# Edge attention of a graph network: scores spread as rows of 512 edges, maxima of two heads at once

## The chip, the cores and the metric

One Trainium2 chip, one of its cores. The metric is the device time of one execution, in microseconds (us).

## The reference, cut to what matters

The program is four stacked graph networks over 3,125 nodes of 128 features (a GAT of three layers, an edge MLP, a GATv2 of two layers, a GCN of two layers). The change lies in the GATv2 alone, whose layer is:

```
xl = (h @ Wl + bl).reshape(N, H, HD); xr = (h @ Wr + br).reshape(N, H, HD)
e = leaky_relu(xl[src] + xr[dst], 0.2)
score = einsum('ehd,hd->eh', e, att)
m = segment_max(score, dst, num_segments=N)
ex = exp(score - m[dst])
den = segment_sum(ex, dst, num_segments=N)
out = segment_sum(ex / (den[dst] + 1e-16) * xl[src], dst, num_segments=N)
```

The reference is given 100,000 edges, sorted by their target `dst`; H is 4 heads, HD 32 features of each.

## The kernel before, in words

Edges are sorted once into NG = 220 groups of 512 edges, each group within one block of 128 target nodes. A group is 4 columns (TG = 4, index `q`) of 128 edges, one edge on each partition. One-hot matrices of the targets lie in memory: `hot` (edges by nodes, fp32) and its transpose `hott` (nodes by edges, bf16).

`gatv2_pass` (from L1575) runs once for each of two layers. Its engines each run their own program through `pipeline` (L103): 8 steps are unrolled in a loop, and a step works on up to six groups at different stages at once, from `edges` (the newest group) over `score`, `maxima`, `merge` and `weights` to `sums` (the oldest). Within a step each engine keeps the order in which its `step` function is written. The engines are tied by semaphores alone.

- **GpSimd** (`gather_rows`, L981): four indirect DMAs (L989), each fetching 128 rows of the source table, for the group 8 places ahead. It waits for `idx_ready`, which ScalarE raises in `next_idx` (L1001) at the end of its step, and for `agg_done`, which TensorE's accumulation raises. **SyncE** loads `hott` and `hot` (L1633, L1634) for the same group behind `agg_done`.
- **TensorE**, in this order: the transpose of the cut scores into `ps_srow` (L1795), which waits for VectorE's `lo_out`; the node maxima at the edges, `ps_node` (L1804); the score products `ps_sc` (L1814); the edge features `ps_e` (three products L1825, four transposes L1829); the spread of the scores for heads 0, 1 and 2 into `ps_top` (L1839); the accumulation `ps_acc` (L1851), which waits for VectorE's `val`; the spread for head 3.
- **VectorE**: `val` (L1665), `faded` (L1670), `there` and `t` (L1679, L1683), `sc` (L1689), maximum of head 0 (L1702), residual `res` (L1712), maximum of head 1, last cut `lo` (L1717), maximum of head 2, the addition to `acc` (L1723), which waits for `agg_done`, maximum of head 3, the new running maximum and its drop (L1729, L1732).
- **ScalarE**: `srow` (L1746) from `ps_srow`, the digits of the targets (L1755), first cut `hi` (L1760), exponential (L1768), second cut `mid` (L1771), which waits for `res`, the relu `bent` (L1777), and the next index copy (L1004).

A maximum for each target node is found so: scores are cut into three bf16 parts (`hi`, `mid`, `lo`), 20 columns each (16 scores, 4 running maxima), and stand beside 64 columns of digits of the targets in one tile `parts` of 128 x 128. Its transpose `srow` has on its partitions all scores and digits of a group. For head h and column q a product with `sel[:, q * HEADS + h, :]` gives for every node and each of the column's 128 edges the score, or the score minus a large number where the edge has another target. The maximum along the 512 edges follows. Three PSUM banks (`TOPS = 3`) take the four heads in turn: head 3 uses head 0's bank again, and head 0 of the next group waits for head 3's maximum. `sel` is made once by GpSimd in `mask_tables` (L1510), beside VectorE's tables of digits, ahead of both layers.

## Time and profile before

| | us |
|---|---|
| median of 3 runs | 9,064.03 |
| lowest, highest | 9,042.72, 9,085.63 |
| profiled execution, its own time | 9,004.81 |
| its span, first to last instruction | 9,003.1 |

In the span, TensorE has matmuls for 5,685.8 us, VectorE is busy for 5,133.5, ScalarE for 2,748.7 and GpSimd for 3,659.2; the mean granted TensorE clock is 0.86 of 2.4 GHz. The two attention passes together lie between 5,238 and 8,509 us of the span. A row of grouped instructions gives line, engine, operation, what it writes and reads, shapes and count, then the busy time and mean of one (ns), then the engine's idle time ahead of them and what ended it. Spans of matmuls overlap, since they are pipelined. A wait for several semaphores is put down to the one that came last by the profile.

### The profile page before, as it was taken

What the parts mean: (1) busy time and instruction counts of PE and PEld (TensorE: products, weight loads), DVE (VectorE), ACT (ScalarE), POOL (GpSimd) and SP (SyncE); (2) the same over time, 40 slices, a digit from 0 to 9 for tenths busy, and PEclk for the clock granted to TensorE, in tenths of its full rate; (3) what the DMA queues carried; (4) which work ended last, traced back from release to release, by engine and by line L of the source; (5) the groups of instructions that cost most, each with busy time, mean ns of one, the idle gap of its engine ahead of it and who ended that gap; (6) DMA issues with size and microseconds to landing.
All of it is one profiled execution on the core that took longest, in us unless ns stands there. A gap on an engine that the chain in (4) does not pass through costs nothing. (4 is left out here: it accounts for less than half of the span.)

```text
span 9003.1 us, 154403 instructions
## 1 busy us (share of the span) xinstructions
PE 5685.8 (63%) x44934; PEld 4616.3 (51%) x44935; DVE 5133.5 (57%) x12349; ACT 2748.7 (31%) x6113; POOL 3659.2 (41%) x3623
## 2 busy tenths in 40 slices
PE   1111117666677775888888357777773777777666
PEld 1000003655577673555555246666662666666566
DVE  7444444999668673333333456666665666666612
ACT  1000000588557552344333212222221222222210
POOL 2666661234000004555555245555551555555300
PEclk9999999888899897898888677888885888888788
DMA  4111113234324223344446023333352333333555
GB/s 159 44 43 43 46 41 139 86 128 140 111 101 156 98 101 85 112 119 118 116 114 105 15 82 93 95 94 98 96 95 47 93 96 95 94 97 96 64 185 191
DMA packets 662769, 884.50 MB, mean 98 GB/s; under 512 B 304425, under 2 KB 487254, under 8 KB 643668
## 3 DMA queue, kind: packets, MB, share of 16 engines
q1 hardware_dynamic: 553028, 674.48, 23.4%
q0 software_dynamic: 109568, 207.74, 11.6%
q8 instruction: 106, 1.74, 0.1%
q14 instruction: 67, 0.55, 0.0%
HBM read 648.77 MB, written 233.08 MB: 98 GB/s over the span
## 5 line engine op out<-in xcount | busy, mean ns | idle before, releaser
L989 POOL DMA_INDIRECT rows<-head_table,idxb x1760 | 1707.7, 970 | 1614.6 <-issue 484.7
L989 POOL DMA_INDIRECT rows<-source_table,idxb x880 | 844.3, 959 | 1800.8 <-ACT idxb L1009 1157.4
L1702 DVE TENSOR_REDUCE gtop<-ps_top 128x1 f32<-128x512 f32 x1760 | 1208.6, 687 | 382.9 <-remote 207.1
L363 POOL DMA_INDIRECT records<-recb,idxb x784 | 768.2, 980 | 440.4 <-issue 372.0
L1839 PE MATMUL ps_top<-srow,sel 128*128 128x128 bf16 x7040 | 668.4, 251 | 297.6 <-DVE gtop L1702 240.2
L1839 PEld LDWEIGHTS ps_top<-srow,sel 128*128 128x128 bf16 x7040 | 549.4, 115 | 401.2 <-DVE gtop L1702 306.5
L391 PE MATMUL ps_g<-hott 64*128 64x128 bf16 x784 | 59.7, 302 | 989.1 <-DVE prior L456 593.8
L1851 PE MATMUL ps_acc<-val,hot 128*128 128x132 f32 x3520 | 615.4, 324 | 95.1 <-issue 72.4
L787 PE MATMUL ps_cells<-hot 128*128 128x128 bf16 x4608 | 481.3, 248 | 255.1 <-DVE hot L745 122.2
L1096 PE MATMUL ps_acc<-rows,pt 128*128 128x128 f32 x3750 | 517.6, 280 | 135.2 <-DVE pt L1117 120.8
L1851 PEld LDWEIGHTS ps_acc<-val,hot 128*128 128x128 f32 x3520 | 532.6, 226 | 131.7 <-issue 101.2
L391 PEld LDWEIGHTS ps_g<-hott 64*128 64x128 bf16 x784 | 35.4, 126 | 1013.4 <-issue 802.2
L1096 PEld LDWEIGHTS ps_acc<-rows,pt 128*128 128x128 f32 x3750 | 462.5, 193 | 168.5 <-DVE pt L1117 161.3
L1814 PE MATMUL ps_sc<-att,bent 128*128 128x4 f32 x3520 | 532.2, 274 | 20.3 <-issue 12.1
L1814 PEld LDWEIGHTS ps_sc<-att,bent 128*128 128x128 f32 x3520 | 506.0, 221 | 34.5 <-issue 13.5
L787 PEld LDWEIGHTS ps_cells<-hot 128*128 128x128 bf16 x4608 | 358.9, 112 | 297.4 <-issue 279.8
L1825 PE MATMUL ps_e<-hott,mine 128*128 128x512 bf16 x1320 | 445.6, 455 | 81.4 <-DMA hot<-one_hots 81.4
L1760 ACT ACTIVATE parts<-sc 128x20 bf16<-128x20 f32 x444 | 97.2, 219 | 1207.6 <-DVE sc L1689 861.7
L729 POOL TENSOR_TENSOR none<-logs,far 128x640 f32<-128x640 f32 x125 | 254.4, 2035 | 499.0 <-ACT logs L819 499.0
L745 DVE TENSOR_TENSOR hot<-hot,pair 128x2048 bf16<-128x2048 bf16 x282 | 409.6, 1506 | 13.4
L1665 DVE TENSOR_TENSOR val<-rows,p 128x528 f32<-128x528 f32 x440 | 309.5, 703 | 186.9 <-issue 186.9
L1461 DVE COPY featt<-ps_featt 64x512 f32<-64x512 f32 x220 | 150.0, 682 | 441.5 <-PE ps_featt L1422 253.6
(327 smaller groups left out, 12548.1 us busy)
## 6 DMA issues: line engine op xcount, KB each, us to landing
logs<-log_counts SPq DMA_DIRECT2D x75, 1600.0 KB
hot<-one_hots SPq DMA_DIRECT2D x440, 256.0 KB
wt<-edge_weights SPq DMA_DIRECT2D x50, 1600.0 KB
one_hots<-hot SPq DMA_DIRECT2D x220, 256.0 KB
hott<-one_hots_t SPq DMA_DIRECT2D x440, 128.0 KB
edge_weights<-both SPq DMA_DIRECT2D x125, 320.0 KB, 2.8
log_counts<-none SPq DMA_DIRECT2D x125, 320.0 KB, 2.2
records<-blank SPq DMA_DIRECT2D x16, 1870.0 KB
```

What stands on the lines that cost most here:

```text
L363: g.indirect_dma_start(out=recs[:, :], out_offset=bass.IndirectOffsetOnAxis(ap=idxb[k][:, t:t + 1], axis=0), in_=recb[k][:, t, :], in_offs ...
L729: g.tensor_tensor(none[r][:, :, :], logs[r][:, :, :], far[r][:, :, :], ALU.subtract).then_inc(masked[r], 1)
L745: ins = ve.tensor_tensor(hot[k][:, m, :, :, :], hot[k][:, 1, :, :, :], value, ALU.mult)
L787: pe.matmul(tile[:, 0:P], hot[k][:, 0, j // 2, :, j % 2], hot[k][:, m, j // 2, :, j % 2], start=False, stop=m == 4, skip_group_check=True)
L989: g.indirect_dma_start(out=rows[r][:, k, :], out_offset=None, in_=table, in_offset=bass.IndirectOffsetOnAxis(ap=idxb[r][:, k:k + 1], axis= ...
L1096: ins = pe.matmul(ps_acc[b % 2][:, 0:D], pt[n % 4][:, t, :], c.rows[:, at, 0:D], start=at == 0, stop=at == NB - 1)
L1665: ve.tensor_tensor(val[k][:, :, :, :], rows[r][:, :, 0:HEADS * HW].rearrange("p q (f h) -> p q f h", h=HEADS), p[k][:, 0:SC].rearrange("p ...
L1702: ve.tensor_reduce(gtop[:, h:h + 1], ps_top[h % TOPS][:, :], AX.X, ALU.max).then_inc(topped, 1)
L1814: ins = pe.matmul(ps_sc[:, q * HEADS:(q + 1) * HEADS], bent[sr % 2][:, q * P:(q + 1) * P], att4[:, :], start=True, stop=True)
L1825: pe.matmul(ps_e[:, :], c.mine[:, bass.ds(b, 1), m, :].rearrange("p a f -> p (a f)"), hott[r][:, :], start=m == 0, stop=False)
L1839: ins = pe.matmul(ps_top[h % TOPS][:, q * P:(q + 1) * P], c.sel[:, q * HEADS + h, :], srow[:, :], start=True, stop=True)
L1851: ins = pe.matmul(ps_acc[:, 0:HEADS * HW], hot[r][:, q, :], val[k][:, q, :, :].rearrange("p f h -> p (f h)"), start=q == 0, stop=q == TG - 1)
```

## The change

A column of scores is given 28 partitions of its own: `parts` becomes 5 strips (4 columns and the running maxima) of 32, each with 12 score columns (3 cuts of 4 heads) and 16 digits. Four transposes lay the four columns side by side, so that `srow` is 28 rows of 512 edges; the other partitions are cleared once and stay zero. One product of 512 columns for each head spreads them, with `sel[:, h, :]`, and no longer four of 128. `ps_top` has all four heads; two heads are one turn, with one signal and one VectorE maximum over 2 x 512. All spreads come ahead of the accumulation, and both maxima, the running maximum and its drop ahead of the addition. TensorE does the score products ahead of the node maxima, and both share a bank, `ps_sn`. `sel` is a quarter as large.

```
-    TOPS = 3
+    PAIR = 2
+    TURNS = HEADS // PAIR
+    NODE = 64
...
-        parts = [sb(f"parts{k}", [P, P], BF16) for k in range(2)]
+        parts = [sb(f"parts{k}", [P, TG + 1, STRIP], BF16) for k in range(2)]
...
-        srow = sb("srow", [P, P], BF16)
+        srow = sb("srow", [P, GE], BF16)
...
-        ps_sc = pb("ps_sc", [P, 512])
+        ps_sn = pb("ps_sn", [P, 512])
         ps_srow = pb("ps_srow", [P, 1024], BF16)
-        ps_top = [pb(f"ps_top{k}", [BN, 512]) for k in range(TOPS)]
-        ps_node = pb("ps_node", [P, 512])
+        ps_top = pb("ps_top", [BN, HEADS, 512])
...
# VectorE
-                        def top(h):
-                            ve.wait_ge(tops, HEADS * mg + (h + 1))
-                            if h == 0:
+                        def top(a):
+                            ve.wait_ge(tops, TURNS * mg + (a + 1))
+                            if a == 0:
                                 wait(ve, newtop, mg)
-                            ve.tensor_reduce(gtop[:, h:h + 1], ps_top[h % TOPS][:, :], AX.X, ALU.max).then_inc(topped, 1)
+                            ve.tensor_reduce(gtop[:, a * PAIR:(a + 1) * PAIR], ps_top[:, a * PAIR:(a + 1) * PAIR, :], AX.X, ALU.max) \
+                                .then_inc(topped, 1)
                         if maxima:
                             top(0)
...
                         if maxima:
                             top(1)
                         if score or merge:
                             ve.wait_ge(mid_out, n + 1)
-                            ve.tensor_tensor(lo, res[:, :], mid, ALU.subtract).then_inc(lo_out, 1)
+                            ve.tensor_tensor(lo, left, mid, ALU.subtract).then_inc(lo_out, 1)
                         if maxima:
-                            top(2)
+                            ve.wait_ge(topped, TURNS * mg + TURNS)
+                            ve.scalar_tensor_tensor(new, last, reset, gtop[:, :], ALU.add, ALU.max).then_inc(newtop, 1)
+                            ve.wait_ge(newtop, mg + 1)
+                            wait(ve, p_ready, mg - 3)
+                            ve.scalar_tensor_tensor(t[mr % 4][:, SC:CUT], last, reset, new, ALU.add, ALU.subtract).then_inc(drop_ready, 1)
                         if sums:
...
-                        if maxima:
-                            top(3)
-                            ve.wait_ge(topped, HEADS * mg + HEADS)
-                            ve.scalar_tensor_tensor(new, last, reset, gtop[:, :], ALU.add, ALU.max).then_inc(newtop, 1)
-                            ve.wait_ge(newtop, mg + 1)
-                            wait(ve, p_ready, mg - 3)
-                            ve.scalar_tensor_tensor(t[mr % 4][:, SC:CUT], last, reset, new, ALU.add, ALU.subtract).then_inc(drop_ready, 1)
# ScalarE
-                            wait(act, tops, HEADS * mg)
-                            act.activation(srow[:, :], ps_srow[:, 0:P], ACT.Copy).then_inc(srow_out, 1)
+                            wait(act, tops, TURNS * mg)
+                            act.activation(srow[0:USED, :], ps_srow[0:USED, 0:GE], ACT.Copy).then_inc(srow_out, 1)
# TensorE
-                            pe.transpose(ps_srow[:, 0:P], parts[mr % 2][:, :], c.identb[:, :]).then_inc(srow_ready, 1)
...
                             for q in range(TG):
...
+                                ins = pe.transpose(ps_srow[0:USED, q * P:(q + 1) * P], parts[mr % 2][:, q, 0:USED], c.identb[:, :])
+                            ins.then_inc(srow_ready, 1)
                         if score:
                             si, sr, _ = score
                             sg = RING * si + sr
                             pe.wait_ge(bent_ready, sg + 1)
                             wait(pe, sc_out, sg)
+                            wait(pe, summed, sg - 3)
...
+                            pe.wait_ge(lo_out, g + 3)
+                            wait(pe, summed, g)
+                            pe.wait_ge(sc_out, sg if score else NG)
+                            for q in range(TG):
+                                ins = pe.matmul(ps_sn[:, NODE + q * PARTS * HEADS:NODE + (q + 1) * PARTS * HEADS],
+                                                hott[r][:, q * P:(q + 1) * P], parts[r % 2][0:BN, TG, 0:PARTS * HEADS],
+                                                start=True, stop=True)
+                            ins.then_inc(at_edges, 1)
...
-                        def spread_scores(heads):
-
-                            for h in heads:
-                                wait(pe, topped, HEADS * mg + (h + 1 - TOPS if h else 0))
-                                for q in range(TG):
-                                    ins = pe.matmul(ps_top[h % TOPS][:, q * P:(q + 1) * P], c.sel[:, q * HEADS + h, :],
-                                                    srow[:, :], start=True, stop=True)
-                                ins.then_inc(tops, 1)
                         if maxima:
                             pe.wait_ge(srow_out, mg + 1)
-                            spread_scores((0, 1, 2))
+                            for a in range(TURNS):
+                                wait(pe, topped, TURNS * (mg - 1) + (a + 1))
+                                for h in range(a * PAIR, (a + 1) * PAIR):
+                                    ins = pe.matmul(ps_top[:, h, :], c.sel[:, h, :], srow[:, :], start=True, stop=True)
+                                ins.then_inc(tops, 1)
                         if sums:
...
-                        if maxima:
-                            spread_scores((3,))
```

In `mask_tables` the selects work on 4 x 128 columns and not on 16 x 128, there is one select for each of the three digits (before: one for each digit and column, 12), and one more memset:

```
-                        for q in range(TG):
-                            part = c.sel[:, q * HEADS:(q + 1) * HEADS, :].rearrange("p h (a n i) -> p (h a) n i", n=values, i=inner)
-                            ins = g.affine_select(out=part, in_=part, compare_op=ALU.not_equal, fill=0.0, base=-64 - q * DIG - at,
...
+                        part = sel.rearrange("p h (a n i) -> p (h a) n i", n=values, i=inner)
+                        count(g.affine_select(out=part, in_=part, compare_op=ALU.not_equal, fill=0.0, base=-PARTS * HEADS - at,
```

## Rows read from the trace of the kernel before

**Rows 1.** Grouped instructions between 5,400 and 6,800 us, shapes apart; 200 steps.

```profile
L1702 DVE TENSOR_REDUCE gtop<-ps_top 128x1 f32<-128x512 f32 x799 | 548.9, 687 | 178.5 <-remote 102.5 <-PE ps_top L1839 49.8 <-issue 22.7
...
L1777 ACT ACTIVATE bent<-ps_e 128x512 f32<-128x512 f32 x198 | 118.1, 596 | 0.0
...
L1723 DVE TENSOR_TENSOR acc<-faded,ps_acc 128x132 f32 x200 | 57.6, 288 | 106.3 <-DMA one_hots<-hot 93.4 <-PE ps_acc L1851 9.7 <-issue 0.8
```

**Rows 2.** Timeline of one step: start, length, engine, line, operation, idle time before.

```profile
6318.34 1.03 PE L1814 MATMUL ps_sc<-att,bent 128*128 128x4 f32 x8
...
6319.22 0.81 PE L1825 MATMUL ps_e<-hott,mine 128*128 128x512 bf16 x3
...
6319.87 0.60 PE L1829 MATMUL ps_e<-ident,rows 128*128 128x128 f32 x4
6320.09 0.29 DVE L1723 TENSOR_TENSOR acc<-faded,ps_acc 128x132 f32 x1 [0.79 <-DMA one_hots<-hot]
6320.27 0.28 ACT L1746 ACTIVATE srow<-ps_srow 128x128 bf16<-128x128 bf16 x1 [2.12 <-remote]
...
6321.04 0.84 PE L1839 MATMUL ps_top<-srow,sel 128*128 128x128 bf16 x12 [0.58 <-DVE gtop L1702]
...
6321.51 0.70 DVE L1665 TENSOR_TENSOR val<-rows,p 128x528 f32<-128x528 f32 x1
...
6322.26 1.17 PE L1851 MATMUL ps_acc<-val,hot 128*128 128x132 f32 x8 [0.38 <-issue]
...
6322.86 0.69 DVE L1702 TENSOR_REDUCE gtop<-ps_top 128x1 f32<-128x512 f32 x1
...
6323.61 0.40 PE L1839 MATMUL ps_top<-srow,sel 128*128 128x128 bf16 x4 [0.18 <-issue]
...
6324.39 0.23 PE L1795 MATMUL ps_srow<-identb,parts 128*128 128x128 bf16 x1 [0.38 <-issue]
...
6326.56 0.29 DVE L1723 TENSOR_TENSOR acc<-faded,ps_acc 128x132 f32 x1 [1.64 <-DMA one_hots<-hot]
6326.74 0.28 ACT L1746 ACTIVATE srow<-ps_srow 128x128 bf16<-128x128 bf16 x1 [2.20 <-remote]
```

**Rows 3.** Timeline of GpSimd alone, 6,314 to 6,356 us.

```profile
6320.84 0.94 POOL L989 DMA_INDIRECT rows<-head_table,idxb  x1 [1.69 <-DMA one_hots<-hot]
...
6324.59 0.94 POOL L989 DMA_INDIRECT rows<-head_table,idxb  x1 [0.30 <-issue]
6327.31 0.94 POOL L989 DMA_INDIRECT rows<-head_table,idxb  x1 [1.78 <-DMA one_hots<-hot]
...
6340.22 0.94 POOL L989 DMA_INDIRECT rows<-head_table,idxb  x1 [1.76 <-DMA one_hots<-hot]
...
6354.64 0.94 POOL L989 DMA_INDIRECT rows<-head_table,idxb  x1 [4.66 <-ACT idxb L1004]
```

**Rows 4.** Who waited for whom, both passes: us in total, times, longest.

```profile
POOL rows L989 <- DMA one_hots<-hot: 311.5, 184, 1.9
...
PE ps_top L1839 <- DVE gtop L1702: 240.2, 264, 17.3
```

**Rows 5.** Timeline of the step that ends at 6,344 us.

```profile
6341.73 1.17 PE L1851 MATMUL ps_acc<-val,hot 128*128 128x132 f32 x8 [0.47 <-issue]
...
6344.51 0.29 DVE L1723 TENSOR_TENSOR acc<-faded,ps_acc 128x132 f32 x1
```

**Rows 6.** Grouped instructions, 5,000 to 5,240 us: VectorE additions from PSUM.

```profile
L965 DVE TENSOR_TENSOR other<-lin_po,add 128x128 f32<-128x128 f32 x40 | 11.7, 292 | 11.6 <-PE lin_po L942 10.3
...
L965 DVE TENSOR_TENSOR rows<-lin_po,brow 128x256 f32<-128x256 f32 x25 | 10.6, 424 | 9.2 <-PE lin_po L942 7.8
```

**Rows 7.** Timeline of the tables' stage, 5,095 to 5,165 us.

```profile
5105.48 41.18 POOL L1542 TENSOR_SCALAR_AFFINE_SELECT sel<-sel 128x512 bf16<-128x512 bf16 x12
...
5128.90 4.42 DVE L1567 TENSOR_SCALAR reset<-reset 128x220 f32<-128x220 f32 x1
5146.81 6.31 POOL L1547 TENSOR_SCALAR_AFFINE_SELECT sel<-sel 128x2048 bf16<-128x2048 bf16 x3
```

69 lines of the change are left out of this document (34 added, 35 removed).

## The prediction

> **What bounds the kernel now.** I read the grouped instructions of the attention pass first, then who waits for whom, then one stretch of the timeline. The pass runs twice, 440 steps of 512 edges. In a stretch of 1400 us there are 200 steps [rows 1], 7.0 us each, or 3,080 us in all. No engine fills a step. VectorE's four maxima take 2.75 us (4 x 687 ns) and its product 0.70; TensorE's spans in one step, 1.03 + 0.81 + 0.60 + 0.84 + 1.17 + 0.40, make 4.9 us with their overlaps [rows 2]; GpSimd starts its four gathers 1.25 us apart, 5.0 us in all.
>
> What the reader is to see is in the timeline. The last accumulating products start at 6322.26 and cover 1.17 us, so by the record they end at 6323.43. VectorE, which waits for exactly those, starts its addition only at 6326.56, and ScalarE, which waits for the transpose recorded at 6324.39, starts at 6326.74 [rows 2]. VectorE lay idle 1.64 us before. So word from TensorE arrived about 3 us late. It arrived 0.95 us and more after GpSimd's fourth gather had ended (6324.59 + 0.94 = 6325.53). The step before and the one after look the same: groups of gathers start at 6320.84, 6327.31 and, the third after the first, 6340.22 [rows 3], 6.46 us apart. This is a **locked cycle**: word of the products, 0.77 us to the first gather, 4.69 us of gathers, about 1.0 us more until TensorE's next word gets through. The waits carry the name of an old DMA, because a wait for several semaphores is put down that way. GpSimd waited in this manner 184 times [rows 4], so I count 184 locked steps out of 440.
>
> The Trainium skill, Perfetto Trace Analysis, section on the Tensor Engine Instruction, says that a matmul's reported end is an estimate, and that the semaphore goes out only when PSUM has acknowledged the writes. The trace agrees, with 3.1 us between the two at 6323.43.
>
> Once the word got through early: products from 6341.73 for 1.2 us, addition already at 6344.51 [rows 3, 5]. The next four gathers then followed without a pause (GpSimd was busy until 6354.64 - 4.66 = 6349.98), and the group after began at 6354.64. Two steps took 14.42 us where two locked ones take 12.92. Finishing early is punished here.
>
> **The change, part by part.**
>
> *Maxima.* A maximum over 512 numbers takes 687 ns. Additions from PSUM take 292 ns for 128 columns and 424 ns for 256 [rows 6], 1.03 ns a column and 160 ns fixed; 687 less 512 columns leaves the same 160. Two heads at once: 160 + 1,055 = 1,215 ns. Two of them are 2.43 us, 0.32 us less a step. Bounds: nothing saved (each inner row pays the fixed part), and 0.32. The Trainium skill, VectorE: DVE Perf Modes, in its errata section, gives 120 cycles fixed for a PSUM source; by that the saving is an estimated 0.25 us. I take 0.32.
>
> *Products that spread the scores.* Twelve of 128 columns take 0.84 us and four 0.40: 55 ns each, and 0.18 us that a burst has once; sixteen stream 0.88 us. Three of 512 columns take 0.81 us: less 0.18, 0.21 each, so four stream 0.84 us [rows 2]. Nothing gained in streaming. The twelve weight loads that fall away lay under matmuls. The Trainium skill, TensorE: Matmul & The Clock Gate, under Back-to-back issue gap, gives 81 ns a matmul at 128 columns and 131 at 512; by that the spread would shrink by an estimated 0.77 us.
>
> *Transposes.* One becomes four, each streaming 128 columns: 3 x 55 ns, 0.17 us more (0.33 at half clock).
>
> *Copy to the score rows.* 128 columns took 0.28 us [rows 2]; the new one has 512 columns on 28 partitions. The relu of 512 columns from PSUM took 596 ns [rows 1]. So 0.32 us more on ScalarE; bounds 0 and 0.32. It lies on the path: the spread waits for it.
>
> *Order.* The fourth head's spread left TensorE after the accumulation, and its maximum left VectorE between the addition and the next product. With it go the running-maximum pieces (2 x 0.22). In both passes TensorE's spread waited for a maximum 264 times, 240.2 us [rows 4]. Now VectorE does both maxima ahead of the addition. But the last cut of the scores, which the next transpose waits for, comes after two long maxima and not after two short ones: 2.43 - 1.37 = 1.06 us later within a step. The chain cut, transpose, score products, edge products, first pair, maximum, cut is then: 0.3 + 1.0 + 0.1 + 1.3 + 0.6 + 1.22 + 1.22 + 0.2 = 5.9 us at full clock, against 0.1 + 1.0 + 0.1 + 1.3 + 0.4 + 1.4 + 0.2 = 4.5 before. ScalarE's middle part and, behind it, the next index copy wait for the residual after the first maximum, 0.53 us later; GpSimd waits for that copy at the end of eight gathers. The scores' products ahead of the node products, and the shared bank's two added waits, are for things a step old: nothing, while VectorE is less than a step behind.
>
> *The tables before the pass*, once: GpSimd works until 5153.12, its 12 selects taking 41.2 us; VectorE beside it is done at 5133.32 [rows 7]. After: two memsets and one select at a quarter of the columns, three of the 3.4 us selects, three small ones: 14 to 23 us. VectorE becomes the end, 19.8 us saved. The new clearing of the row buffer costs under 1 us a pass.
>
> **A locked step with the change**, on the clock of rows 2. Word arrives about 6320.07, VectorE adds at 6320.09 and can start the product at 6320.35 instead of 6321.51; it ends at 6321.05. ScalarE's copy, from 6320.27, ends at 6320.87 instead of 6320.55. The spread runs 6320.91 to 6321.77 and the accumulation to 6322.89, against 6323.43. That is 2.05 us behind the first gather instead of 2.59. Does the word then get through? At 6341.73 + 1.17 = 6342.90, 2.68 us behind the first gather, it did, by 6344.51; at 2.59 it did not. TensorE's words at 1 to 2 us behind a first gather do arrive (the spread of 6321.04 was read by a maximum at 6322.86, with the gather from 6320.84 running). So I take it that 2.05 gets through more often than 2.59, and that locked steps turn into pairs of eight gathers. A pair costs 14.42 + 0.53 = 14.95 us, 2.03 above two locked steps. All 184 locked steps as 92 pairs: +187 us. After a pair the chain above is late and an ordinary step follows, so I take half: +93. Steps that are not locked (256) gain from the order and lose by the chain of 5.9 us, which half clock lengthens; I put them at zero, between -0.49 and +0.3 us each. With -20 for the tables: **+73 us**.
>
> Against its own profiled run, 9,004.8 us (span 9,003.1), the sum gives 9,078; the median of the runs is 9,064, 59 us higher, so I forecast **9,137 us**.
>
> **Rivals.**
> *The lock holds.* The accumulation's word still waits for the gathers; every edit hides behind it, and VectorE waits longer. For it: 6.46 us came out three times running, however the work within fell. Against: the early word of rows 5. Time: 9,064 - 20 = 9,044. Chance 0.28.
> *Faster: the late word has nothing to do with the gathers, or the unlocked steps decide.* Then the accumulation's start 0.49 us earlier (6321.77 against 6322.26) moves the whole step, and I let it count in half of the 440: 440 x 0.49 / 2 = 108, with 20 for the tables: 8,936. It decides from the point where the word comes within a few tenths of the recorded end in most steps. For it: TensorE's wait for the maxima is real, 240.2 us. Against: the regular 6.46. Chance 0.28.
> *The spread does become cheaper.* If four products of 512 columns streamed as fast as four of 128 do (0.40 - 0.18 = 0.22 us, not 0.84), unlocked steps would be up to 0.62 us shorter: 9,064 - 256 x 0.62 - 20 = 8,885. The edge products of the same width, 0.21 us each, speak against it [rows 2]. Chance 0.02. This is where the rule on the issue gap would lead.
>
> **How the numbers follow.** Forecast (pairs and the longer chain) 0.42, its own range 9,070 to 9,270 (all pairs, plus some of the unlocked steps at +0.3). Half a percent, 45 us, is about what a measurement of this kernel can tell from no change. Faster by more than that: 0.30. Within: 0.28. Slower: 0.42. The range from 8,910 to 9,270 leaves out the cheap spread, the tail of the faster case and steps worse than all pairs, about 2 in 10.
>
> **What would show it.** Right: maxima of two heads near 1.22 us, copy near 0.6 us, transposes 4 to a step; gather runs of eight more common, fewer waits of VectorE's addition, more of GpSimd for the index copy and of ScalarE for the transpose. The tables' stage ends about 20 us sooner. Wrong: gather groups still mostly 6.46 us apart with longer idle time ahead of the addition (lock holds), or groups 5 to 6 us apart with no long ones behind them (faster).

## The result and the profile after the change

The change made the kernel slower: 9,469.56 us (median of 4 runs, 9,460.68 to 9,480.49) against 9,053.38 for the kernel before (4 runs beside them), a ratio of 1.0456, 95% interval 1.0422 to 1.0489. The forecast was 9,137 with a range up to 9,270: slower, as forecast, but by 416 us where 73 were forecast. The profiled execution has a span of 9,459.0 us against 9,003.1.

The grouped instructions of the whole kernel after the change, as on its page (busy time, mean of one, idle time before them):

```profile
L989 POOL DMA_INDIRECT rows<-head_table,idxb x1760 | 1687.0, 959 | 2121.0 <-ACT idxb L1004 1401.3
L1703 DVE TENSOR_REDUCE gtop<-ps_top 128x2 f32<-128x1024 f32 x880 | 1075.2, 1222 | 948.0 <-PE ps_top L1843 730.9
...
L1797 PE MATMUL ps_srow<-identb,parts 128*28 128x128 bf16 x1760 | 197.0, 242 | 965.0 <-DVE parts L1721 948.3
```

The sizes of single instructions came out near what was forecast. The maximum over two heads takes 1,222 ns (1,215 forecast), and VectorE's maxima in all take 1,075 us against 1,209 (1,760 of 687 ns). The work is less and the wait in front of it more: 948 us. The transposes, now four to a step, wait 948 us for line 1721, the last cut of the scores.

Who waited for whom in both passes of the kernel after (total, times, longest), against [rows 4]:

```profile
POOL rows L989 <- ACT idxb L1004: 1401.3, 391, 32.4
ACT parts L1772 <- DVE res L1715: 1059.3, 348, 4.7
PE ps_srow L1797 <- DVE parts L1721: 948.3, 413, 12.1
...
DVE gtop L1703 <- PE ps_top L1843: 730.9, 314, 3.2
```

Read as one loop (a word is the semaphore signal by which an engine tells another that its result is there): VectorE waits for the spread products, TensorE for the last cut, which is VectorE's, and GpSimd and ScalarE for what stands behind the first maximum. The wait of VectorE's addition for the accumulation [rows 1] is gone; "acc" waited 7.7 us in all. All of the loss lies in this pass: VectorE's first addition at line 1731 starts at 5,274.2 and the last of 440 at 8,965.4, 3,691 us apart, where the kernel before has 5,285.2 and 8,508.3, 3,223 us apart. That is 468 more, or 1.06 us for each of 440 steps.

GpSimd alone, the first gather of each group of four (the fences leave out the three that follow 0.30 us behind one another), against [rows 3]:

```profile
6189.33 0.94 POOL L989 DMA_INDIRECT rows<-head_table,idxb  x1 [3.06 <-ACT idxb L1004]
...
6196.73 0.94 POOL L989 DMA_INDIRECT rows<-head_table,idxb  x1 [2.72 <-ACT idxb L1004]
...
6205.53 0.94 POOL L989 DMA_INDIRECT rows<-head_table,idxb  x1 [4.11 <-ACT idxb L1004]
...
6213.64 0.94 POOL L989 DMA_INDIRECT rows<-head_table,idxb  x1 [3.42 <-ACT idxb L1004]
```

The groups start 7.4, 8.8 and 8.1 us apart, not 6.46, and none of these follows another without a pause. Counted over both passes, GpSimd paused for more than 0.6 us ahead of 391 groups of gathers before the change and ahead of 424 after it. So the pairs of eight gathers that I forecast became rarer and are not what cost the time here. One step of this trace:

```profile
6302.08 0.94 POOL L989 DMA_INDIRECT rows<-head_table,idxb  x1 [2.68 <-ACT idxb L1004]
...
6305.04 1.91 PE L1843 MATMUL ps_top<-srow,sel 128*128 128x512 bf16 x4
...
6305.82 0.94 POOL L989 DMA_INDIRECT rows<-head_table,idxb  x1 [0.30 <-issue]
...
6307.90 1.23 DVE L1703 TENSOR_REDUCE gtop<-ps_top 128x2 f32<-128x1024 f32 x1 [3.18 <-PE ps_top L1843]
...
6309.04 0.17 DVE L1715 TENSOR_TENSOR res<-sc,parts 128x20 f32<-128x20 f32 x1
6309.13 1.22 DVE L1703 TENSOR_REDUCE gtop<-ps_top 128x2 f32<-128x1024 f32 x1
...
6310.26 0.17 DVE L1721 TENSOR_TENSOR parts<-res,parts 128x20 bf16<-128x20 f32 x1
...
6310.56 0.60 PE L1797 MATMUL ps_srow<-identb,parts 128*28 128x128 bf16 x4 [2.69 <-DVE parts L1721]
...
6310.94 0.94 POOL L989 DMA_INDIRECT rows<-head_table,idxb  x1 [4.17 <-ACT idxb L1004]
```

Two things are in it. The word of the spread products is late: four products are recorded up to 6306.95 (the two of the first pair up to 6306.10), and the maximum of the first pair begins at 6307.90, 1.1 us after the fourth gather ended. And behind that word stand two maxima of 1.22 us, then the cut, then the next transposes. My first theory joined the two: the late word, and the long row of work behind it.

The tables' stage did better than forecast. From GpSimd's first instruction (5104.59) to SyncE's load of the weights (5134.09) it takes 29.5 us; before, from 5098.87 to 5154.01, 55.1. The select at line 1536, three digit selects (10.50 us) and three small ones (5.96) are done at 5123.91, and VectorE sets the end. 25.6 us saved, against 19.8 forecast.

### The profile page after: what moved, and what is told of

The parts are those of the page before. It is cut to its first block and busy times, and to the rows that moved or that the text cites. A ratio compares the mean times of both kernels' runs of the same rounds, so it can differ in the third digit from the quotient of the medians.

```text
span 9459.0 us, 144173 instructions
## 1 busy us (share of the span) xinstructions
PE 5817.7 (62%) x40641; PEld 4492.6 (47%) x40975; DVE 5055.4 (53%) x11471; ACT 2874.9 (30%) x6113; POOL 3609.0 (38%) x3614
## 5 line engine op out<-in xcount | busy, mean ns | idle before, releaser
L1703 DVE TENSOR_REDUCE gtop<-ps_top 128x2 f32<-128x1024 f32 x880 | 1075.2, 1222 | 948.0 <-PE ps_top L1843 730.9
L1797 PE MATMUL ps_srow<-identb,parts 128*28 128x128 bf16 x1760 | 197.0, 242 | 965.0 <-DVE parts L1721 948.3
L1843 PE MATMUL ps_top<-srow,sel 128*128 128x512 bf16 x1758 | 667.0, 521 | 14.4 <-issue 12.9
L1851 PEld LDWEIGHTS ps_acc<-val,hot 128*128 128x128 f32 x3520 | 555.9, 222 | 128.8 <-issue 62.8
L1797 PEld LDWEIGHTS ps_srow<-identb,parts 128*28 128x28 bf16 x1760 | 108.9, 102 | 1057.4 <-DVE parts L1721 872.4
L1806 PE MATMUL ps_sn<-att,bent 128*128 128x4 f32 x3520 | 590.6, 291 | 20.2 <-issue 20.2
L1806 PEld LDWEIGHTS ps_sn<-att,bent 128*128 128x128 f32 x3520 | 552.2, 239 | 78.9 <-issue 44.3
L1851 PE MATMUL ps_acc<-val,hot 128*128 128x132 f32 x3520 | 541.2, 303 | 12.8 <-DVE val L1666 11.0
L1772 ACT ACTIVATE parts<-res 128x20 bf16<-128x20 f32 x444 | 97.1, 219 | 1349.3 <-DVE res L1715 1059.3
L1833 PEld LDWEIGHTS ps_e<-ident,rows 128*128 128x128 f32 x1760 | 326.4, 197 | 172.8 <-issue 121.5
```

The lines of the kernel that those rows point to most:

```text
L1703: ve.tensor_reduce(gtop[:, a * PAIR:(a + 1) * PAIR], ps_top[:, a * PAIR:(a + 1) * PAIR, :], AX.X, ALU.max) \
L1797: ins = pe.transpose(ps_srow[0:USED, q * P:(q + 1) * P], parts[mr % 2][:, q, 0:USED], c.identb[:, :])
L1806: ins = pe.matmul(ps_sn[:, q * HEADS:(q + 1) * HEADS], bent[sr % 2][:, q * P:(q + 1) * P], att4[:, :], start=True, stop=True)
L1833: ins = pe.matmul(ps_e[:, q * P:(q + 1) * P], rows[r][:, q, 0:D], c.ident[:, :], is_transpose=True, start=False, stop=q == TG - 1)
L1843: ins = pe.matmul(ps_top[:, h, :], c.sel[:, h, :], srow[:, :], start=True, stop=True)
L1851: ins = pe.matmul(ps_acc[:, 0:HEADS * HW], hot[r][:, q, :], val[k][:, q, :, :].rearrange("p f h -> p (f h)"), start=q == 0, stop=q == TG - 1)
```

## The experiments

**How the numbers stand to one another.** The experiments were measured in five sets, each beside its own runs of the kernel before. In three sets that kernel took 9,023, 9,064 and 9,071 us, near the 9,053 of the comparison above, and in two 7,773 and 7,769. So only ratios within a set are compared. What differs can be seen in the traces. In the sets near 7,770 TensorE's word goes out at the recorded end of its products while a gather runs; I call these sets with prompt words, the others sets with late words. The kernel after shows it: VectorE lay idle for more than 0.3 us ahead of a maximum 383 times in after_third (prompt), and each of these maxima began 0.04 us after the recorded end of the product that gives the word; in the trace above (late) it was 368 times, half of them 1.38 us or more after that end, at most 3.8. The kernel after, with prompt words (after_third, timeline, part of a step):

```profile
6268.19 1.29 PE L1843 MATMUL ps_top<-srow,sel 128*128 128x512 bf16 x4
6268.30 0.94 POOL L989 DMA_INDIRECT rows<-head_table,idxb  x1 [0.30 <-issue]
...
6269.09 1.22 DVE L1703 TENSOR_REDUCE gtop<-ps_top 128x2 f32<-128x1024 f32 x1 [2.30 <-PE ps_top L1843]
...
6269.54 0.94 POOL L989 DMA_INDIRECT rows<-head_table,idxb  x1 [0.30 <-issue]
```

The first pair's maximum begins 0.90 us after the first of the four products did, inside a gather (6268.30 to 6269.24); in the trace above it was 2.86 us, and after the last gather. A part of that difference is TensorE's clock: the four products took 1.91 us there and 1.29 here. In plain_after below, which has no gathers, a step with products of 1.91 us has 1.09 us.

The recorded expectations name these cases. The theory is the late word together with the long row behind it. Rival 1: TensorE's spread and its transposes cost more than priced. Rival 2: only the index copy's lateness counts. Rival 3: spreading all heads ahead of the accumulation is what costs. Theory A says that the late words carry the loss, theory B that the cut behind two long maxima does, with or without late words.

| kernel | edit | words in its set | us | ratio to before | 95% |
|---|---|---|---|---|---|
| after (shown first) | | late | 9,470 | 1.0456 | 1.0422 to 1.0489 |
| after_again | none | late | 9,329 | 1.0359 | 1.0328 to 1.0390 |
| after_third | none | prompt | 8,191 | 1.0544 | 1.0526 to 1.0562 |
| before_again, _third, _fourth | before, unaltered | late | 9,016 to 9,079 | 0.9996 to 1.0004 | within 0.998 to 1.002 |
| cut_early | residual, maximum, last cut, maximum | prompt | 7,794 | 1.0028 | 1.0017 to 1.0039 |
| cut_early_again | the same | prompt | 7,799 | 1.0036 | 1.0022 to 1.0050 |
| lo_early | maximum, residual, last cut, maximum | late | 9,146 | 1.0082 | 1.0054 to 1.0110 |
| idx_early | index copy ahead of the middle part | prompt | 8,172 | 1.0508 | 1.0491 to 1.0526 |
| spread_late | second pair spread behind the accumulation | prompt | 8,406 | 1.0815 | 1.0797 to 1.0833 |
| plain_before | before, no gathers in the pass | late | 8,231 | 0.9133 | 0.9107 to 0.9159 |
| plain_after | after, no gathers in the pass | late | 8,691 | 0.9636 | 0.9604 to 0.9668 |
| single | one maximum a head | prompt | 7,684 | 0.9888 | 0.9872 to 0.9905 |
| single_again | the same | prompt | 7,690 | 0.9891 | 0.9874 to 0.9907 |
| single_third | the same | late | 9,068 | 1.0003 | 0.9989 to 1.0017 |
| single_cut | single and the order of cut_early | prompt | 7,819 | 1.0060 | 1.0043 to 1.0077 |
| single_idx | single and idx_early | late | 9,094 | 1.0021 | 1.0006 to 1.0036 |
| old_order | new layout, old order, one maximum a head | late | 9,052 | 0.9976 | 0.9961 to 0.9990 |

**cut_early and cut_early_again.** The residual goes ahead of the first fused maximum, the last cut behind it.

```diff
                         if score or merge:
...
-                        if maxima:
-                            top(0)
                             ve.tensor_tensor(left, ..., hi, ALU.subtract).then_inc(res_ready, 1)
                         if maxima:
-                            top(1)
+                            top(0)
                         if score or merge:
                             ve.wait_ge(mid_out, n + 1)
                             ve.tensor_tensor(lo, left, mid, ALU.subtract).then_inc(lo_out, 1)
+                        if maxima:
+                            top(1)
```

> Theory (late word and long cut): TensorE's word of the spread products comes about 1 us after GpSimd's four gathers have ended, and behind it the kernel after the change puts one maximum of 1.22 us before the residual, the middle part and the next index copy, and two of them before the last cut that the next transpose waits for. With the residual ahead of the first maximum and the last cut behind one maximum, the index copy comes about 1.3 us sooner and the cut 1.2 us sooner; 1.0 us in most of 440 steps: 9,030 to 9,150 us, and GpSimd's waits for the index copy fall from 391 to under 200. Rival 1 (the spread and its four transposes cost more on TensorE than priced): within 40 us of 9,470, since no TensorE work moves. Rival 2 (only the index copy's lateness counts, not the cut's): the same as a kernel with the index copy moved alone, 9,200 to 9,300.

> Two fused maxima, the last cut behind the first, the residual ahead of it, repeated. Theory: 1.003 where words don't stay out, as measured; where they do, the residual, the middle part and the index copy no longer stand behind the held word of the spread, so 0.96 to 1.01, 8,700 to 9,150 us. Rival (held words decide, whatever the order on VectorE): 1.03 to 1.05.

Measured 1.0028 and 1.0036, with prompt words, where the kernel after measures 1.0544: moving two instructions of 0.17 us on VectorE gives back 392 of 422 us (8,191 to 7,799, in one set). Rival 1 (TensorE's work) falls, rival 2 (the index copy) with idx_early below, and so does the rival that puts all on the late words, since there were none. This kernel was not measured with late words; lo_early, below, stands in for it.

**idx_early.** The index copy moves ahead of ScalarE's wait for the residual.

```diff
+                        if sums:
+                            next_idx(act, c, idxb, idx_ready, rows_in, sums[0], sums[1])
                         if score or merge:
                             act.wait_ge(res_ready, n + 1)
...
-                        if sums:
-                            next_idx(act, c, idxb, idx_ready, rows_in, sums[0], sums[1])
```

> The index copy alone moves ahead of ScalarE's wait for the residual. Theory (late word and long cut): GpSimd no longer waits for the first maximum, the residual and the middle part (about 1.22 + 0.3 + 0.3 us), but the next transpose still waits for two maxima, so the chain that sets the step stays at nearly its length: 9,300 to 9,420. Rival 2 (only the index copy's lateness counts): nearly the whole loss back, 9,030 to 9,150. Rival 1 (TensorE's work): 9,430 to 9,510, GpSimd's idle time moves to another wait.

1.0508 against 1.0544: 19 us of 422 by the times, 28 by the ratios, both with prompt words but in two sets. GpSimd's waits in the attention passes, after_third first, then idx_early:

```profile
POOL rows L989 <- ACT idxb L1004: 608.9, 360, 5.5
```

```profile
POOL rows L989 <- PE ps_acc L1851: 406.8, 153, 7.1
...
POOL rows L989 <- ACT idxb L1004: 134.1, 121, 2.9
```

The largest wait of GpSimd, the one for its index copy, was a symptom: with the copy early GpSimd waits for the accumulation instead, and the pass is nearly as long (2,974 us from the first addition to the last, against 2,987). The size is nearest to rival 1's and not my theory's (1.03 to 1.04 by its times), though cut_early excludes rival 1's reason. What this edit alone is worth with late words was not measured.

**single, single_again, single_third.** One maximum per head, one word of TensorE per head; the last cut behind the second of four.

```diff
-    PAIR = 2
+    PAIR = 1
...
                             ve.tensor_tensor(lo, left, mid, ALU.subtract).then_inc(lo_out, 1)
+                        if maxima:
+                            top(2)
+                            top(3)
```

> One maximum per head again (four of 687 ns, a word from TensorE for each head), the last cut behind the second of them, the residual behind the first; all four heads are still spread ahead of the accumulation. Theory (late word and long cut): the cut comes 1.07 us sooner within the step and the index copy 0.53 us, VectorE works 0.3 us longer; in most of 440 steps 0.6 to 0.9 us: 9,070 to 9,210. Rival 3 (spreading all heads ahead of the accumulation is what costs): within 60 us of 9,470 or slower. Rival 1 (TensorE's work): 9,470 plus up to 130 for VectorE's 0.3 us.

> The kernel with one maximum per head, the last cut behind the second, repeated. Theory (the chain from cut to cut is the loss): most of the loss back in either condition, a ratio to the kernel before of 0.98 to 1.01 where words stay out (8,850 to 9,150 us), 0.985 to 0.992 where they don't. Rival (where words stay out, the spread of all heads ahead of the accumulation holds them longer): 1.02 or more there.

> The kernel with single maxima again: 0.989 of the kernel before, as twice measured, where words don't stay out; where they do, 0.98 to 1.01 (theory) or 1.02 and more (rival: held words make the spread of all heads ahead of the accumulation costly).

With prompt words 0.989, twice: more than the whole loss back, and 1.1% faster than the kernel before (I had expected 9,070 to 9,210 us beside a kernel of 9,053, ratios of 1.002 to 1.017). With late words 1.0003. VectorE works longer in this version than in the kernel after (four times 685 ns against twice 1,222), and is faster for it. VectorE's waits for the spread products in the two attention passes, after_third first, then single, both with prompt words:

```profile
DVE gtop L1703 <- PE ps_top L1843: 602.3, 380, 4.2
```

```profile
DVE gtop L1703 <- PE ps_top L1846: 70.2, 42, 4.7
```

532 us less waiting, and 507 us less time (8,191 to 7,684, in two sets). Against cut_early, which took 110 us more in the same set as single, two things differ, a maximum and a word for each head and the residual's place; the runs don't fully part them.

**spread_late.** The second pair of heads is spread behind the accumulation.

```diff
-                            for a in range(TURNS):
+                            for a in range(1):
...
                             ins.then_inc(agg_done, 1)
+                        if maxima:
+                            for a in range(1, TURNS):
+                                wait(pe, topped, TURNS * (mg - 1) + (a + 1))
+                                for h in range(a * PAIR, (a + 1) * PAIR):
+                                    ins = pe.matmul(ps_top[:, h, :], c.sel[:, h, :], srow[:, :], start=True, stop=True)
+                                ins.then_inc(tops, 1)
```

> The second pair of heads is spread after the accumulation, as the fourth head was before. Theory (late word and long cut): the second maximum, and behind it the last cut and the next transpose, must wait for a word that comes behind the accumulation, 0.6 us or more later: 9,550 to 9,750. Rival 3 (spreading all heads ahead of the accumulation is what costs): 9,100 to 9,300. Rival 1 (TensorE's work in amount, not order): within 40 us of 9,470.

1.0815, slower than the kernel after (after_third) by 0.027 of the kernel before, some 210 us. I expected 80 to 280 us above the kernel after, and this lies within. Spreading all heads ahead of the accumulation is no cause of the loss (rival 3 falls); with the cut behind the second maximum it keeps the loss from being larger.

**after_again, after_third; before_again, before_third, before_fourth.** Both kernels unaltered.

> The first four experiments ran beside a kernel before of 7,773 us, where the first comparison had 9,053, and the traces looked at so far show TensorE's words there at the recorded ends of its products, gathers running or not. This run repeats the kernel after the change unaltered. Theory A (the late words carried the loss): without them the loss shrinks to less than half, a ratio of 1.00 to 1.02, or 7,780 to 7,930 us. Theory B (the cut behind two long maxima is a chain of its own, 5.9 us against 4.5 as priced, and decides also without late words): by the four experiments the kernel lies 400 or so above the one with the cut early (7,794) and above the one with the index copy early (8,172): 8,170 to 8,350, a ratio of 1.05 to 1.07.

> The kernel after the change once more, so that the runs of this call have it beside them. The two calls before this differed: beside the first four experiments the kernel before took 7,773 us and TensorE's words went out at their recorded ends with gathers running; in the other call, and in the runs shown first, it took 9,023 and 9,053 and the words stayed out while gathers ran. Theory: the loss is 1.03 to 1.05 where words stay out (9,300 to 9,500), and where they don't it is larger, not smaller, since the chain from cut to cut (5.64 us without gathers, against 4.75) then sets every step: 1.06 to 1.10, 8,230 to 8,550. Rival (the late words carry the loss): 1.00 to 1.02 where they don't stay out.

> The kernel before unaltered, for its trace beside the other runs of this call: 7,773 us within 0.3%. Theory A and B both expect its accumulation's word within 0.2 us of the recorded end, steps of 5.5 to 6 us instead of 7.0, and GpSimd's four gathers, 5.0 us, as the next limit.

> The kernel before unaltered, for its trace beside these runs: 7,769 us within 0.3% or, where TensorE's words stay out while gathers run, 9,020 to 9,060. Theory: where they don't stay out its steps are 4.9 to 5.3 us at full clock, set by four gathers (5.0) and a chain of 4.75, against 5.64 after the change.

> The kernel before unaltered, for its trace: 7,770 us where TensorE's words go out at the recorded ends; steps of 4.9 to 5.3 us at full clock there, with GpSimd's gathers back to back (5.0 us), a chain of 4.75 hidden behind them, against 5.64 after the change; or about 9,050 where the words stay out.

The change costs 3.6 to 4.6% with late words and 5.4% with prompt ones (my range for that said 6 to 10). So the late words don't carry the loss: theory A and the rival that follows it fall. All traces of the kernel before came with late words; what its step looks like with prompt ones was not seen.

**plain_before and plain_after.** Indexed gathers replaced by plain loads on SyncE's queue, in this pass alone. Every group then gets the first 128 rows of the table, not its own, so the results are others.

```diff
-                @block.gpsimd
-                def _(g):
-                    gather_rows(g, table, rows, idxb, idx_ready, rows_in, agg_done, begun)
...
                         sp.sem_inc(begun, 1)
+                        for k in range(TG):
+                            sp.dma_start(rows[r][:, k, :], table[0:P, :]).then_inc(rows_in[r], 16)
```

> The kernel before with the indexed gathers of the attention pass (not of the other passes) replaced by plain loads of the table's first 128 rows on the SyncE queue, so GpSimd does nothing in this pass; the rows are the wrong ones, so the output is not the reference's, and the loads wait for no index copy. Theory B: the step is then the chain of TensorE, ScalarE and VectorE, 4.5 us or what SyncE's six issues take (some 0.5 us each, 3 us): 440 x (5.6 - 4.7) = 400 us less than the kernel before, 7,300 to 7,500. If the gathers were not the limit: within 60 us of 7,773.

> The kernel after with the same replacement of the gathers (output not the reference's). Theory B: the longer chain from cut to cut stays, 5.9 us against 4.5, so this is 350 to 650 us above the same edit of the kernel before. Theory A, or that the loss is only made where GpSimd waits for its index copy: within 100 us of the edited kernel before, or below it, since VectorE's maxima take 0.32 us less a step.

Without gathers the kernels lie 8,691 - 8,231 = 461 us apart, much as with them (416 and 305 with late words, 422 with prompt ones). This is the plainest run of the study: the loss needs no gathers. The late words do: in plain_after VectorE waited 383 times for the spread products, and each wait ended 0.04 us after their recorded end, in a set in which the kernel before took 9,023 us. (For plain_before I had expected 7,300 to 7,500 us, 270 to 470 below a kernel of 7,773; it lay 793 below one of 9,023.) As nothing is held up here, the step can be read. First the kernel before without gathers, from one last cut (6318.01) to the next (VectorE's and TensorE's lines; idle time of under 0.2 us isn't printed):

```profile
6318.01 0.17 DVE L1715 TENSOR_TENSOR parts<-res,parts 128x20 bf16<-128x20 f32 x1
6318.09 0.68 DVE L1700 TENSOR_REDUCE gtop<-ps_top 128x1 f32<-128x512 f32 x1
...
6318.23 0.23 PE L1793 MATMUL ps_srow<-identb,parts 128*128 128x128 bf16 x1
...
6318.69 0.28 DVE L1721 TENSOR_TENSOR acc<-faded,ps_acc 128x132 f32 x1
...
6318.89 0.69 DVE L1700 TENSOR_REDUCE gtop<-ps_top 128x1 f32<-128x512 f32 x1
...
6320.10 0.70 DVE L1663 TENSOR_TENSOR val<-rows,p 128x528 f32<-128x528 f32 x1
...
6320.52 0.83 PE L1837 MATMUL ps_top<-srow,sel 128*128 128x128 bf16 x12
...
6321.45 0.69 DVE L1700 TENSOR_REDUCE gtop<-ps_top 128x1 f32<-128x512 f32 x1
...
6322.75 0.17 DVE L1715 TENSOR_TENSOR parts<-res,parts 128x20 bf16<-128x20 f32 x1
```

4.74 us, and VectorE has no pause of more than 0.12 us in it: it is the limit. While TensorE makes its round (transpose, scores, edges, spread), VectorE does two maxima, the addition, the product and the small sums. The same stretch of the kernel after:

```profile
6307.27 0.17 DVE L1719 TENSOR_TENSOR parts<-res,parts 128x20 bf16<-128x20 f32 x1
...
6307.49 0.40 PE L1795 MATMUL ps_srow<-identb,parts 128*28 128x128 bf16 x4
...
6308.09 0.70 DVE L1664 TENSOR_TENSOR val<-rows,p 128x528 f32<-128x528 f32 x1
...
6308.83 0.81 PE L1827 MATMUL ps_e<-hott,mine 128*128 128x512 bf16 x3
...
6309.91 1.03 PE L1841 MATMUL ps_top<-srow,sel 128*128 128x512 bf16 x4
...
6310.55 1.22 DVE L1701 TENSOR_REDUCE gtop<-ps_top 128x2 f32<-128x1024 f32 x1 [1.02 <-PE ps_top L1841]
...
6311.77 1.22 DVE L1701 TENSOR_REDUCE gtop<-ps_top 128x2 f32<-128x1024 f32 x1
...
6312.91 0.17 DVE L1719 TENSOR_TENSOR parts<-res,parts 128x20 bf16<-128x20 f32 x1
...
6313.13 0.40 PE L1795 MATMUL ps_srow<-identb,parts 128*28 128x128 bf16 x4 [1.29 <-DVE parts L1719]
```

5.64 us: 3.28 from the cut until the first pair can be reduced (6307.27 to 6310.55), 2.36 for two maxima with the cut behind them. No maximum is left to fill the 3.28 us, so VectorE idles 1.02 us and TensorE 1.29. In these two stretches the step differs by 0.90 us. The pass as a whole grew by more: the first and last addition are 2,487.4 us apart in the one (5,267.6 to 7,755.0) and 2,963.9 in the other (5,260.2 to 8,224.1), 476 us more. Counted over both passes, 354 of the 442 stretches from one last cut to the next in plain_before have the full granted clock throughout, and their median is 4.82 us; in plain_after 237 have it, with a median of 5.64: 0.82 us a step. All stretches together take 2,370 us in the one and 2,855 in the other, 485 us more, or 1.10 us a step. An estimate from these numbers: 442 x 0.82 = 362 us for the chain if all steps ran at full clock. What remains is in steps during which TensorE's clock was low for a part; plain_after has 205 of them, plain_before 88. How much of it the clock makes by itself isn't shown. In both kernels one of these steps comes once in eight, as often as the loop turns: 9.0 to 9.5 us in plain_before, about 8.0 in plain_after. In plain_before TensorE stands still there ahead of its transpose:

```profile
6307.13 0.28 PE L1793 MATMUL ps_srow<-identb,parts 128*128 128x128 bf16 x1 [3.60 <-issue]
```

The next fences are of the view by windows: the stretch, its length, the busy times of TensorE, its weight loads, VectorE, ScalarE and GpSimd with their counts, the granted clock, DMA's share, GB/s. Of plain_after, most of the step before the one above, and that one:

```profile
6301.60:6307.30 5.70, 5.70 (x24) 3.85 (x24) 2.88 (x7) 1.20 (x5) 0.00 (x0) 0.52 0.14 45
6307.30:6312.90 5.60, 4.42 (x36) 3.34 (x35) 4.44 (x13) 1.96 (x7) 0.00 (x0) 1.00 0.45 120
```

The transposes of the step before started at 6299.75, behind an idle time of TensorE of 1.88 us; the next set came 7.74 us later, most of it at a granted clock of 0.52, that is nearly all at 1.2 GHz, against 5.64 us at 1.00 (2.4 GHz). From the first addition to the last the clock is 0.85 in plain_after and 0.91 in plain_before. TensorE's idle time ahead of its transposes is 519.6 us in plain_after, with a median of 1.29 us, and 302.2 us in plain_before, mostly 0.38 us or none, but over 3 us in 51 steps. With gathers and late words the clock is 0.77 after the change and 0.81 before, the kernel after first:

```profile
5280.00:8960.00 3680.00, 2561.31 (x15075) 1873.64 (x15294) 2034.69 (x5359) 868.11 (x3115) 1652.93 (x1724) 0.77 0.34 79
```

```profile
5290.00:8505.00 3215.00, 2425.31 (x19248) 2000.65 (x19246) 2107.61 (x6237) 742.76 (x3120) 1674.40 (x1725) 0.81 0.39 91
```

**lo_early.** The smallest edit: only the last cut moves, between the two fused maxima.

```diff
                             ve.tensor_tensor(left, ..., hi, ALU.subtract).then_inc(res_ready, 1)
-                        if maxima:
-                            top(1)
-                        if score or merge:
                             ve.wait_ge(mid_out, n + 1)
                             ve.tensor_tensor(lo, left, mid, ALU.subtract).then_inc(lo_out, 1)
+                        if maxima:
+                            top(1)
```

> The kernel after with one edit: the last cut stands between the two fused maxima; the residual stays behind the first. Theory (the chain from cut to cut): 1.22 us off the chain, so most of the loss back: 0.99 to 1.01 of the kernel before. The kernel with the residual moved ahead as well measured 1.003. Rival (the residual's place did it): 1.03 to 1.05.

1.0082 with late words, where the kernel after measured 1.0359 and 1.0456 in two other sets: three quarters or more of the loss comes back, by one instruction. It confirms the cut's place as the cause with late words too, and shows that the residual's place is not needed for most of it. The rest, 0.8%, is left open.

**old_order.** New tables and layout, but the kernel before's order of spreads, maxima and addition, and one maximum a head (`PAIR = 1`). TensorE's score products stay ahead of the node maxima.

```diff
-                            for a in range(TURNS):
+                            for a in range(3):
...
+                        if maxima:
+                            for a in range(3, TURNS):
+                                wait(pe, topped, TURNS * (mg - 1) + (a + 1))
+                                for h in range(a * PAIR, (a + 1) * PAIR):
+                                    ins = pe.matmul(ps_top[:, h, :], c.sel[:, h, :], srow[:, :], start=True, stop=True)
+                                ins.then_inc(tops, 1)
```

(and on VectorE `top(3)` and the running maximum behind the addition)

> The kernel after with single maxima and the order of the kernel before: three heads spread ahead of the accumulation, the fourth behind it, its maximum behind VectorE's addition. Only the layout is new: wide score rows, four transposes, one product per head, the shared bank. Theory: the new layout costs little and the new order brings the gain that single maxima show (0.989), so 1.00 to 1.01 here. Rival (the gain is the layout's): 0.985 to 0.992.

0.9976, between the two ranges: 22 us less than before by the ratio, about what the tables' stage saves. So with late words the wide score rows, the four transposes, the longer copy of ScalarE and the shared bank cost nothing that shows in a step. That single_third gave 1.0003 in the same set says that the new order gains nothing with late words; whether the 1.1% with prompt words is the order's is not shown, as this kernel has no run with prompt words.

**single_cut and single_idx.** Two tries at a version that beats both.

```diff
-                        if maxima:
-                            top(0)
                             ve.tensor_tensor(left, ..., hi, ALU.subtract).then_inc(res_ready, 1)
                         if maxima:
-                            top(1)
+                            top(0)
...
                         if maxima:
+                            top(1)
                             top(2)
                             top(3)
```

> Both edits together: one maximum per head, the residual ahead of the first, the last cut behind the first. Theory: the chain loses a further 0.69 us against the single maxima with the old place of the cut; where words don't stay out GpSimd's gathers (5.0 us a step) already set nearly all steps, so within 50 us of the kernel with single maxima; where words stay out it is the fastest of the four, 0.95 to 0.99 of the kernel before, 8,600 to 8,950 us. Rival: within 40 us of the single maxima in both conditions.

> Single maxima, and the next index copy ahead of the middle part. Theory: where words go out in time, the index copy hides behind the gathers and nothing changes against the single maxima alone: 0.985 to 0.992 of the kernel before. Where they stay out, an earlier index copy lets more groups of four gathers follow without a pause, and the words in between stay out for both: 1.00 to 1.02. Rival (GpSimd's 576 us of waiting for the index copy in that condition is time that can be had): 0.96 to 0.985 there.

(single_idx is single with the edit of idx_early.) single_cut missed my range: 129 us above single_again, not within 50. VectorE's waits of that run between 4,700 and 7,200 us suggest the price:

```profile
DVE res L1713 <- ACT parts L1763: 124.4, 419, 0.4
```

The residual now stands in front of everything, and ScalarE's first part isn't ready: 0.30 us, 419 times, on an engine that single keeps busy. cut_early, with the same order, has the same line with 128.7 us. single_idx, 1.0021 with late words, gains nothing over single_third, though GpSimd's wait for its index copy fell from 610 to 236 us.

## Why the prediction was right in direction and wrong in size

*Maxima, copy, spread, transposes, tables.* Right or near: 1,222 ns against 1,215; 586 ns for ScalarE's copy against near 600; four products of 512 columns 1.03 us by the record at full clock against 0.84 plus the burst's 0.18; tables 25.6 against 19.8 us. The layout doesn't move the pass with late words, as old_order shows. The maxima shrank by 4 x 687 - 2 x 1,222 = 304 ns a step; my 0.32 us was nearer than the estimate of 0.25 from the Trainium skill's 120 cycles (VectorE: DVE Perf Modes, errata). The spread got 0.20 us cheaper by the record, 1.03 us at full clock against 0.83 and 0.40 in plain_before for the old twelve and four, which is about the 0.18 us of one burst the fewer. The 0.77 us that I estimated from the Trainium skill's issue gaps (TensorE: Matmul & The Clock Gate, Back-to-back issue gap) did not come.

*Order.* The failing step. I worked out the chain from cut to cut, 5.9 us against 4.5 before, and then did not let it count: the 256 steps outside the lock were "put at zero, between -0.49 and +0.3 each". Measured without gathers the chain is 5.64 us, against a step of 4.74 that VectorE sets: +0.90 in the stretches shown, +0.82 by the medians of all steps at full clock, near three times the upper bound I gave. Over all steps the mean grew by 1.10 us, and it was not confined to 256 of them. The bound +0.3 had no row behind it. What I missed in it is that the order of VectorE's work, not its sum, was the matter: before, two of four maxima (1.37 us) stood behind the cut and filled TensorE's round; after, none did. Fusing saved 0.3 us of VectorE's work, and the new order put 1.02 us of idle time into its step. The 5.9 us itself was close to the 5.64 measured.

*The locked cycle.* I held the step for set by gathers and late words. They do add time (plain_before is 793 us faster), but they add it to both kernels. As a forecast of the change the lock was the wrong place to look: the loss is of one size, 305 to 461 us, with words late, with words prompt, and with no gathers at all. The 3.1 us that I read between a recorded end and its reader is hardly an error of the recorded ends: in the kernel after, with prompt words or without gathers, the waiting reader starts 0.04 us behind them. The working of the locked step has a slip besides: 6321.77 and the 1.17 us of the accumulation make 6322.94, not 6322.89; no step of the argument hangs on 0.05 us.

*Locked steps become pairs of eight gathers, +93 us.* Wrong for this kernel, which has fewer pairs than the one before; of use for one that I didn't forecast. A short chain with late words does it: single_third, GpSimd alone, first gathers of the groups that had to wait:

```profile
6164.17 0.98 POOL L989 DMA_INDIRECT rows<-head_table,idxb  x1 [1.76 <-DMA one_hots<-hot]
...
6178.78 0.94 POOL L989 DMA_INDIRECT rows<-head_table,idxb  x1 [4.88 <-ACT idxb L1004]
```

Between the two, eight gathers run through, and two steps take 14.61 us. GpSimd paused ahead of 352 groups there, against 391 in the kernel before. That single's gain of 1.1% goes this way when words are late fits, but wasn't tested by itself. I applied the cost of finishing early to a kernel that finishes late. So the direction of my forecast was luck: it was slower for another reason than the one that I added up.

*Index copy, 0.53 us later.* It was put into the pairs. Measured alone, with prompt words: 19 us.

*Clock.* The text said that half clock lengthens the chain and gave it no number. Without gathers, some 120 of the 485 us (485 less 362) are left for it and for the turns of the loop together, by estimate; the runs don't part the two.

*Rivals.* "The lock holds" (9,044) and "faster" (8,936) both fell; the cheaper spread too. None of my cases said that VectorE's order alone, with no gather in it, would set the step; that case, priced from my own two chains at (5.9 - 4.5) x 440, would have given 616 us, too much by a third or more.

## What to carry to other kernels

When two engines hand work back and forth once a step, write down for each hand-over what the other engine does meanwhile. Fusing two instructions saves their fixed part, but removes a place between them where a short instruction could have gone, and here the last cut of the scores needed that place. If a chain comes out longer than the work of the busiest engine, count it in every step, and test it by moving the one short instruction before trusting the largest wait in the profile: that wait (for the index copy, 609 us with prompt words and 1,401 with late ones) was worth 19 us where it was tried, with prompt words.

## What the runs showed of the hardware

The same kernel before took 7,769 to 7,773 us in two sets of runs and 9,023 to 9,071 in three, between which nothing in the program differed. With it goes a delay of TensorE's semaphores while GpSimd issues indexed gathers. In the kernel after, the maximum that waits for the spread products starts 0.04 us after their recorded end in the one kind of set, and up to 3.8 us after it in the other, in the step shown 1.1 us behind the end of the fourth gather; with the gathers taken out (plain_after) it is 0.04 us there too. What sets which of the two comes stays open. A ratio in one kind of set need not hold in the other: the single maxima are worth 1.1% with prompt words and nothing with late ones.

In this pass TensorE's granted clock stood at 1.00 in a step of 5.64 us, and at 0.52 in most of one that followed an idle time of 1.88 us and took 7.74; a chain longer by 0.82 us a step at full clock made the mean step 1.10 us longer without gathers.

A maximum over 2 x 512 columns took 1,222 ns and two over 512 took 2 x 687: the fixed part, some 160 ns, was paid once.
